# Routing of a mixture-of-experts layer: places singly between wide matmuls, column numbers written turned, all comparisons in one go, second products behind them

## The reference, cut to what matters

```python
scores = jax.nn.sigmoid(x @ gate_w.T) + bias
topk_w, topk_idx = jax.lax.top_k(scores, TOPK)                 # 4 of 16
topk_w = topk_w / (jnp.sum(topk_w, axis=-1, keepdims=True) + 1e-20)
cw = jnp.sum(jax.nn.one_hot(topk_idx, E, dtype=x.dtype) * topk_w[..., None], axis=1)
g = jnp.einsum('th,eih->eti', x, Wg)
u = jnp.einsum('th,eih->eti', x, Wu)
z = jax.nn.silu(g) * u
zw = z * cw.T[:, :, None]
out = jnp.einsum('eti,ehi->th', zw, Wd)
out = out + jax.nn.silu(x @ Sg.T) * (x @ Su.T) @ Sd.T          # shared expert
```

## Time and profile before

| | |
|---|---|
| Median of 3 runs | 1751.92 us (1749.41 to 1754.07) |
| The profiled execution's own time | 1754.08 us |
| Its span, first to last instruction | 1752.3 us |
| PE busy | 1687.3 us, 96% |
| DVE busy | 1286.9 us, 73% |
| ACT busy | 920.7 us, 53% |
| POOL busy | 952.1 us, 54% |
| Mean granted clock of PE | 0.990 of full speed |

### The profile page before, as it was taken

How to read it: one execution, slowest core, us unless ns; L and a number is a source line. 1 busy time by engine, 2 the same in 40 slices (tenths; PEclk the granted TensorE clock), 3 DMA queues, 4 the chain that set the end, 5 groups by cost and what they waited for, 6 DMA issues and landing times. The chain is left out here.

```text
span 1752.3 us, 39049 instructions
## 1 busy us (share of the span) xinstructions
PE 1687.3 (96%) x15461; PEld 962.8 (55%) x15461; DVE 1286.9 (73%) x2062; ACT 920.7 (53%) x1518; POOL 952.1 (54%) x871
## 2 busy tenths in 40 slices
PE   7899999799999999999999999999889999999997
PEld 5666665455555555555555555555455555455553
DVE  6777777888888888888888888888785444344445
ACT  7676774656464645455555555565643333333334
POOL 5556664456464636465555556464634555455545
PEclk9999999999999999999999999999999999999999
DMA  5431323112212314132222132131267778877658
GB/s 164 132 86 35 79 62 81 61 57 89 69 65 73 109 43 145 44 101 93 73 74 97 37 98 71 37 109 37 82 224 217 143 147 224 242 189 150 117 97 300
DMA packets 88897, 190.68 MB, mean 109 GB/s; under 512 B 14800, under 2 KB 33744, under 8 KB 86672
## 3 DMA queue, kind: packets, MB, share of 16 engines
q1 hardware_dynamic: 65232, 130.72, 22.3%
q0 software_dynamic: 22912, 57.32, 16.1%
q10 hardware_dynamic: 576, 0.14, 0.0%
HBM read 124.95 MB, written 63.21 MB: 107 GB/s over the span
## 5 line engine op out<-in xcount | busy, mean ns | idle before, releaser
L1151 POOL TENSOR_TENSOR xa_sc<-xa_sc,xa_rs 128x1024 f32<-128x1024 f32 x32 | 60.8, 1901 | 366.4 <-DVE xa_rs L1415 366.4
L1139 POOL TENSOR_TENSOR xa_xs<-xa_xs,sn 128x512 f32<-128x512 f32 x160 | 227.8, 1424 | 52.1 <-ACT xa_xs L1221 52.1
L297 PE MATMUL bank<-xhl,front_h 128*128 128x512 f16 x640 | 244.7, 382 | 11.7 <-DVE front_l L679 9.8
L298 PE MATMUL bank<-xhl,front_h 128*128 128x512 f16 x640 | 244.5, 382 | 0.0
L299 PE MATMUL bank<-xhl,front_l 128*128 128x512 f16 x640 | 244.0, 381 | 0.0
L1146 POOL TENSOR_TENSOR xa_rr<-xa_x,xa_xs 128x512 f32<-128x512 f32 x156 | 232.0, 1487 | 17.9 <-DVE xa_x L1373 2.5
L297 PE MATMUL bank<-out_h,xa_oh 128*128 128x512 f16 x512 | 195.0, 381 | 12.9 <-DVE out_l L1418 5.2
L2195 POOL DMA_INDIRECT scratch_y<-raw_front,moe_to x79 | 125.3, 1585 | 149.8 <-DVE mo_zl L2249 118.6
L298 PE MATMUL bank<-out_l,xa_oh 128*128 128x512 f16 x512 | 194.7, 380 | 0.0
L299 PE MATMUL bank<-out_h,xa_ol 128*128 128x512 f16 x512 | 194.6, 380 | 0.0
L1220 ACT ACTIVATE xa_xs<-bank 64x512 f32<-64x512 f32 x160 | 95.0, 593 | 133.2 <-PE bank L299 117.7
(11 more groups left out here) (320 smaller groups left out, 4667.3 us busy)
## 6 DMA issues: line engine op xcount, KB each, us to landing
xa_rawc<-in_ew SPq DMA_DIRECT2D x32, 768.0 KB, 5.3
moe_ring<-scratch_w SPq DMA_DIRECT2D x16, 1536.0 KB, 8.8
scratch_w<-xa_chunk_h SPq DMA_DIRECT2D x32, 384.0 KB, 2.3
scratch_w<-xa_chunk_l SPq DMA_DIRECT2D x32, 384.0 KB, 3.3
raw_front<-in_xwq SPq DMA_DIRECT2D x8, 1024.0 KB, 7.9
raw_out<-in_xwo SPq DMA_DIRECT2D x8, 1024.0 KB, 5.8
scratch_y<-acc SPq DMA_DIRECT2D x6, 1024.0 KB, 6.3
acc<-in_x POOLq DMA_DIRECT2D x4, 1024.0 KB, 7.8
```

The costliest lines, as they stand in the source:

```text
L297: pe.matmul(out_ap, ah, bh, start=start and m == 0, stop=False)
L298: pe.matmul(out_ap, ah, bl, start=False, stop=False)
L1139: PO.mark(pool.tensor_tensor(xr, xr, sn[:, :].rearrange("p (a s) -> p a s", a=1) .to_broadcast([P, QT // S, S]), ALU.mult), f"sm{r}", st, ...
L1151: PO.mark(pool.tensor_tensor(s4, s4, rs[:, :, :].rearrange("p h (t a) -> p (h t) a", a=1) .to_broadcast([P, 16, S]), ALU.mult), "nm", st)
```

## The change

- PE no longer does the places of groups 0 to 3 in one block, but one place behind each wide matmul of the second half of `front(1)` (`front_with_places`); those that are left over (8 of 32) follow behind it. In the same way the places of groups 4 to 7 go between the 12 wide matmuls of `y0.2` and `y0.3`, and the 20 that are left follow behind them. `y0.0` and `y0.1` move ahead of all places, `gu1.0` ahead of those.
- `at_col` is laid out with the column as innermost index, so that PE reads it without steps. DVE writes it in the old order of elements, so each element goes 83 elements (166 bytes) on from the last.
- On DVE `w4` moves from ahead of the slots to between `locate(3)` and `locate(4)`, and `products(1)` from between them to behind `own`, that is behind all eight groups.
- The low parts `zl1` move from POOL to DVE, behind the list.
- ACT's program is not touched, nor SP's.

```diff
-            at_row, at_col = ([b(f"{w}{n}", [P, c, NR], F16) for n in range(NB)] for w, c in (("at_row", P), ("at_col", COLS)))
+            at_row = [b(f"at_row{n}", [P, P, NR], F16) for n in range(NB)]
+            at_col = [b(f"at_col{n}", [P, NR, COLS], F16) for n in range(NB)]
...
-                          ["logits"] + quad("gu", 0, IB) + ["counts"] + quad("gu", 1, IB) + several("place", *range(4)) + ["y0.0"]
-                          + several("place", *range(4, 8)) + ["owners", "y0.1", "y0.2", "y0.3", "y1.0", "y1.1", "turn0", "y1.2", "turn1", "y1.3"])
+                          ["logits"] + quad("gu", 0, IB) + ["counts", "gu1.0", "y0.0", "y0.1", "place0", "place1", "gu1.1", "place2", "place3", "y0.2", "place4",
+                                                                "y0.3"] + several("place", *range(5, 8)) + ["owners", "y1.0", "y1.1", "turn0", "y1.2", "turn1", "y1.3"])
...
-                          ["down", "chosen"] + quad("z", 0, IB) + ["w4", "slots"] + several("at", *range(4)) + quad("z", 1, IB)
-                          + several("at", *range(4, 8)) + ["own", "list", "tables", "to", "xl0", "xl1", "ws0", "ws1"])
-            PO = Timeline(sem("ro_pool"), [], 0, [x for q in range(2) for x in quad("zl", q, IB)])
+                          ["down", "chosen"] + quad("z", 0, IB) + ["slots"] + several("at", *range(4)) + ["w4"]
+                          + several("at", *range(4, 8)) + ["own"] + quad("z", 1, IB) + ["list"] + quad("zl", 1, IB) + ["tables", "to", "xl0", "xl1", "ws0", "ws1"])
+            PO = Timeline(sem("ro_pool"), [], 0, quad("zl", 0, IB))
...
-                        i = dve.tensor_tensor(at_col[g % NB][:, :, :], hit[g % 2][:, :, :], along(m.tok_no_h[:, ts], COLS), ALU.mult)
+                        i = dve.tensor_tensor(at_col[g % NB][:, :, :].rearrange("p n c -> p c n"), hit[g % 2][:, :, :], along(m.tok_no_h[:, ts], COLS), ALU.mult)
...
                 locate(0, 1, 2, 3)
-                products(1)
+                then(dve.tensor_reduce(tot[:, :], top8[:, :, 0:TOPK], AX.X, ALU.add))
...
                 locate(4, 5, 6, 7)
...
+                products(1)
                 wait(dve, PE, f"place{PLACES - 1}")
...
+                for n in range(IB):
+                    wait(dve, AC, f"zh1.{n}")
+                    DV.mark(dve.tensor_tensor(zl[1][:, n, :], z[:, n, :], zh[1][:, n, :], ALU.subtract), f"zl1.{n}", N0)
...
+                def places(groups, first, last):
+
+                    for m in range(first, min(last, NR * len(groups))):
+                        place(groups[m // NR], m % NR)
...
+                def front_with_places(q, n, groups):
+
+                    wait(pe, DV, f"z{q - 1}.{n}")
+                    tok, m = slice(q * QT, (q + 1) * QT), 0
+                    for u in range(2):
+                        c, o = u * FI + n * P, bank[2 + 2 * n + u]
+                        for k in range(KD):
+                            h, l = wf_h[:, k, c:c + P], wf_l[:, k, c:c + P]
+                            for w, x in ((h, xh), (l, xh), (h, xl)):
+                                mm = pe.matmul(o[:, :], w, x[:, k, tok], start=k == 0 and w is h and x is xh,
+                                               stop=k == KD - 1 and x is xl, skip_group_check=True)
+                                m += 1
+                                if m == 6 * KD:
+                                    PE.mark(mm, f"gu{q}.{n}", N0)
+                                places(groups, m - 1, m)
+                    places(groups, m, 4 * NR)
...
                         if t >= 2:
                             wait(pe, AC, f"y{q}.{t - 2}")
...
-                front(1)
-                place_picks(0, 1, 2, 3)
-                back(0, 0)
-                place_picks(4, 5, 6, 7)
+                front(1, 0)
+                back(0, 0, 1)
+                front_with_places(1, 1, range(4))
+                back(0, 2, 3, groups=range(4, 8))
                 wait(pe, DV, "own")
                 PE.mark(pe.matmul(bank[1][0:1, 0:NTILES + 2], own_h[:, :], identh[:, 0:NTILES + 2], start=True, stop=True), "owners", N0)
-                back(0, 1, 2, 3)
                 back(1, 0, 1)
```

More of the change, by code:

```diff
@@ L2032, in logits, with place @@
                     return mm
-                def place_picks(*groups):
-                    for g in groups:
+                def place(g, n):
+                    if n == 0:
                         wait(pe, DV, f"at{g}")
[L2037 to L2041, removed]
+                    j, t = g * NR // NT, (g * NR + n) % NT
+                    mm = pe.matmul(bank[0][:, j * COLS:(j + 1) * COLS], at_row[g % NB][:, :, n], at_col[g % NB][:, n, :],
+                                   start=t == 0, stop=t == NT - 1, skip_group_check=True)
+                    if n == NR - 1:
@@ L2042, in place_picks, with front @@
                         PE.mark(mm, f"place{g}", N0)
-                def front(q, ns=range(IB)):
+                def front(q, n):
                     tok = slice(q * QT, (q + 1) * QT)
[L2046 to L2050, removed]
-                            mm = three_pass(pe, bank[2 + 2 * n + u][:, :],
-                                            [(wf_h[:, k, c:c + P], wf_l[:, k, c:c + P], xh[:, k, tok], xl[:, k, tok])
-                                             for k in range(KD)])
-                        PE.mark(mm, f"gu{q}.{n}", N0)
@@ L2056, in back @@
-                def back(q, *ts):
+                    if q:
+                        wait(pe, DV, f"z{q - 1}.{n}")
+                    for u in range(2):
+                        c = u * FI + n * P
+                        mm = three_pass(pe, bank[2 + 2 * n + u][:, :], [(wf_h[:, k, c:c + P], wf_l[:, k, c:c + P], xh[:, k, tok], xl[:, k, tok])
+                                                                       for k in range(KD)])
+                    PE.mark(mm, f"gu{q}.{n}", N0)
+                def places(groups, first, last):
+                    for m in range(first, min(last, NR * len(groups))):
+                        place(groups[m // NR], m % NR)
@@ L2057, in back @@
+                def back(q, *ts, groups=()):
                     if q == 0:
                         wait(pe, DV, "down")
-                    wait(pe, PO, f"zl{q}.1")
+                    wait(pe, DV if q else PO, f"zl{q}.1")
+                    m = 0
                     for t in ts:
@@ L2065, in back @@
                         tok = slice(t * P, (t + 1) * P)
-                        PE.mark(three_pass(pe, bank[6 + t % 2][:, :], [(zh[q % 2][:, n, tok], zl[q % 2][:, n, tok], wo_h[:, n, :], wo_l[:, n, :])
-                                                                       for n in range(IB)]), f"y{q}.{t}", N0)
+                        for n in range(IB):
+                            for a, w in ((zh, wo_h), (zh, wo_l), (zl, wo_h)):
+                                mm = pe.matmul(bank[6 + t % 2][:, :], a[q % 2][:, n, tok], w[:, n, :], start=n == 0 and a is zh and w is wo_h,
+                                               stop=n == IB - 1 and a is zl, skip_group_check=True)
+                                m += 1
+                                if m % (3 * IB) == 0:
+                                    PE.mark(mm, f"y{q}.{t}", N0)
+                                places(groups, m - 1, m)
+                    places(groups, m, 4 * NR)
                 pe.wait_ge(s_gate_v, 2)
@@ L2078, in tensor @@
                 PE.mark(mm, "logits", N0)
-                front(0)
+                front(0, 0)
+                front(0, 1)
                 pe.wait_ge(s_c, 16 * CONSTANTS)
```

12 lines of the change are left out of this document (5 added, 7 removed).

## The result

The changed kernel takes 1776.41 us (median of 4 runs, 1773.78 to 1779.57), the kernel before 1751.88 us in the same job: a ratio of 1.0136, 95% interval 1.0117 to 1.0155. By the medians it is 24.5 us slower; the ratios given here are estimated over the executions, so they can differ a little from the quotient of the medians, here 1.0140. The forecast was 1766 in a range of 1759 to 1772. The direction and the place were right, the size was not: the time lies beyond the upper end.

The account below looks back on a forecast made before the run. It took PE, 96% busy, as the bound, fed by DVE and ACT in the routing stage. The steps put the experts at 1353.3 instead of 1339.4, 13.9 us later; 1751.92 + 13.9 = 1765.8, forecast 1766, range 1759 to 1772.

Parts of the forecast that it names:

- Step 1: DVE slots: w4 leaves the way, 1.02 of 1.87 us gained as POOL holds L1976; first hit at 1312.18.
- Step 2: DVE's turned at_col write: 1.32 us, 0.82 more than before, so a group takes 2.25 us instead of 1.43.
- a step of 166 bytes, not 16: Rival on DVE's turned write: 2.5 ns per element, a group of 2.73 us, +17.8 us, 1769.7; chance 0.15.
- Step 3: DVE from the first hit through eight groups, w4 and own to the end of z1: 1333.04, before 1320.2.
- Step 4: PE up to place 31: pairs 0.253 us, DVE sets the pace, single places 0.15 us, place3 at 1322.6.
- Step 5: New PE wait ahead of y0.2 for ACT's copy of y0.0, behind zh1 and z1: 11.8 us idle.
- Step 6: PE after the idle time: 12 pairs mostly at half clock 5.4 us, 20 single places 3.0, place7 at 1343.0.
- Step 7: From last place to experts: list, gather landing in 4.6 us, y1, turn0; experts at 1353.3, before 11.5 us behind place7.
- My last rival: Not slower, routing stage: tail and interleaving pay for the new wait, giving back up to 6 us, 1746; chance 0.05.

Follow-up runs that it names:

- x7_steps_quiet: Kernel before plus single 256-element DVE writes of various steps, placed where POOL is idle: f16 at step 83 about 1.25 us, f32 at wide step 0.64 us.
- x4: Changed kernel with at_col in the old layout and ACT's copies of y0.0 and y0.1 ahead of zh1: 1754.59 us against 1752.41, ratio 1.0012.
- x10: x4 plus one ACT copy per group that turns at_col into a tile without steps for PE: 1753.14 us against 1753.05, ratio 1.0004.
- x3: Changed kernel, turned write kept, with ACT's copies of y0.0 and y0.1 between si1.0 and si1.1: 1767.32 us against 1754.13, ratio 1.0073.
- x8: x3 with turned at_col written without steps by eight small tensor_scalars a group, hit removed: 1759.15 us, ratio 1.0033.
- x6: Kernel before plus 15 single 256-element DVE instructions of various steps ahead of the groups, some beside POOL's work: f16 at step 83 took 1.27 us.

## Why the forecast was wrong, by its steps

**Step 1 held.** L1970, called L1976 before, was held by POOL: 1.28 us instead of 0.42. The first `hit` came at 1314.81 - 2.66 = 1312.15; forecast 1312.18.

**Step 2 failed, and this is the miss.** "So `at_col` takes 664 x 1.77 ns + 0.15 = 1.32 us", from L2014, "the only row with such a write". It took 2.92 us, and a group 3.77 instead of 2.25: 8 x 1.52 = 12.2 us too little. L2014 writes f32, and x7_steps_quiet shows that this was what mattered: a 4-byte write with a wide step costs (0.64 - 0.14)/256 = 2.0 ns an element, near my 1.77, but a 2-byte one 4.3 ns. I had named the width of the step as the doubt ("a step of 166 bytes, not 16") and bounded it at 2.5 ns. The width was not it: 32 bytes cost what 166 do. The size of the element was, and my bound left it out although the text said that no row showed a 2-byte output. It was the term with the thinnest evidence, multiplied by 8, and the range should have been widest there. The Trainium skill ("Vector Engine (DVE) Microarchitecture Reference", 5.2 Measured stream behaviour on trn2), from which I had the agreeing 1.71 ns, measured 32-bit streams, and for those it is near the 2.0 ns of the probes here; for 16-bit ones the measurement decides.

**Step 3** held but for step 2: `z1` came at 1347.8 - 2.7 = 1345.1 instead of 1333.0, 12 us late, as step 2 alone would have it.

**Step 4 was half right.** Pairs are 0.255 us apart (forecast 0.253), and the clock didn't fall. But single places, "0.15 (bound by the same load)", go at 0.07 us with `at_row` as stepped as ever. The weight load was not what set the pace in the earlier trace rows; the stepped moving operand was, as x4 against x10 shows with the same load in both (0.37 against 0.256 us a pair). So I had also misread: not DVE's 1.43 us a group set the pace of those places, for they go at 5.33/32 = 0.167 us, and the second 32 in the kernel before go at 0.16 us each, the pace of x4, though DVE's last product was done 2 us ahead of the last of them:

```profile
1322.85 5.11 PE L2040 MATMUL bank<-ro_at_col,ro_at_row 128*128 128x83 f16 x32
```

The fast places gave back 1.9 us behind `y0.3`: 1.35 us from 1354.82 to `owners` at 1356.17, where the forecast had 3.2 to `place7`.

**Step 5 had the right mechanism and, through step 2, the wrong size:** 18.1 us idle instead of 11.8, released by the very instruction named. x3 shows it by taking it away: -11 us on the medians. It is less than 18 since in x3 waits for the last groups come in its place (15.5 us of such waits in all, against 8.2 here).

**Step 6 held:** the 12 pairs took 5.8 us (1349.04 to 1354.82), forecast 5.4, at half clock. **Step 7 held:** from the last place to the experts 9.8 us (1356.17 to 1365.97), forecast 10.3, before 11.5, and the gather issued at 1357.88 was there when `turn0` came at 1362.49, 4.6 us later.

The sum: +12.0 at `y0.2`, +0.4 for the pairs, -1.9 for the places, -0.5 for the tail, 10.0 us above the forecast of +13.9. That gives the 23.9 by which the stage is longer; the medians show 24.5.

My last rival ("24 + 12 places hidden under wide matmuls at full clock would give back up to 6 us, 1746") was no true one either. In x4 the waits are gone and the layout is the one that is cheap to write, and it takes 1754.6: there the places don't hide. In x3 and x8 they hide, but are dear to write. x10, with ACT in between, comes nearest to the rival: cheap on DVE, hidden on PE, and it takes 1753.1, as the kernel before, because the list comes no earlier and the first gather later.

## What to carry to other kernels

Before the layout of a tile is turned, price both ends with the element size in hand: a write with a step is paid on DVE for every element, however small it is, and a matmul's moving operand with a step is paid on PE. Bound a cost that no row shows by more than a doubling of the nearest row if that row differs in type, and most of all if the cost is multiplied. And when work is moved past others on one engine, follow what copies and conversions on the idle engines stand behind it: two ACT copies of 0.6 us cost 9 to 11 us here by their place alone.

## What the runs showed of the hardware

- DVE, two inputs, 256 elements of f16: 0.29 us in a row, 0.45 at step 2, 0.59, 0.73, 0.87 at 3, 4, 5, and 1.23 to 1.34 at steps of 8 to 83. f32: 0.43 at steps 1 and 2, 0.64 at 4 to 42. Pairs of f16 84 apart: 0.40. One input read at a step of 8, f16: 0.60; at a step of 4: 0.42 (x6).
- PE, 128 by 83 columns: 0.16 us with a moving operand at a step of 16 bytes, 0.07 us without; behind a wide matmul 0.153 against 0.04 us (0.366 and 0.255 less 0.213). A weight load with that step hides under a wide matmul. Whether it costs anything among single places isn't shown, as no run loads it without a step: such a place goes at 0.07 us, a turn of 128 columns without steps at 0.056.
- ACT copies 664 elements, read at a step of 16 bytes, in 1.43 us on the mean (2.2 ns an element), beside 0.60 us for 512 without a step.
- A `tensor_scalar` of 83 elements with two numbers from memory takes 0.23 us of DVE back to back.
- The granted clock was at 2.4 GHz behind a wait of 3.4 us in the kernel after, and through the next 11 us, in which PE was busy 57% in bursts with waits of 1.5 to 1.8 us. It was at 1.2 GHz behind a wait of 18 us there and behind one of 1.9 us in x4 (0.50 from 1334.40 to 1339.10). In x10, behind the same 1.9 us, it was at 1.00 for 0.8 us and at 0.50 then. So by these rows the length of the last wait alone does not tell the clock.
- A first gather issued about 1 us behind the last weight load landed in 6.2 us (before) and 8.0 us (x10), 0.2 to 0.3 us behind that load each time; issued 4.2 us behind it, in 3.8 us (x4).
